# Cross-attention chain: softmax sums from TensorE and output division in the last four narrow jobs

## What is computed

```python
# layers 0 and 3
xn = rmsnorm(x, norm_w)
q = (xn @ wq).reshape(B, T, N_HEADS, HEAD_DIM)
k = (cond @ wk).reshape(B, S, N_KV_HEADS, HEAD_DIM)
v = (cond @ wv).reshape(B, S, N_KV_HEADS, HEAD_DIM)
scores = jnp.einsum('btgrd,bsgd->bgrts', qg, k) * scale
attn = jax.nn.softmax(scores.astype(jnp.float32), axis=-1).astype(q.dtype)
out = jnp.einsum('bgrts,bsgd->btgrd', attn, v).reshape(B, T, N_HEADS * HEAD_DIM)
return residual + out @ wo
```

## Time and profile before

| | us |
|---|---|
| median of 3 runs | 382.94 |
| lowest of them | 382.5 |
| profiled execution, its own time | 384.65 |
| span of the profiled execution | 382.9 |

### The profile page before, as it was taken

The page is one execution under the profiler, slowest core; times in us unless marked ns, Lnnn a source line. Parts: engine busy times, 40 slices in busy tenths (PEclk is TensorE's granted clock), DMA queues, the critical chain, the costliest instruction groups (busy, mean ns, idle before and its releaser), DMA issues.

```text
span 382.9 us, 10493 instructions
## 1 busy us (share of the span) xinstructions
PE 359.0 (94%) x3522; PEld 319.2 (83%) x3522; DVE 268.5 (70%) x1401; ACT 278.9 (73%) x1176; POOL 187.4 (49%) x220
## 2 busy tenths in 40 slices
PE   6799899999999999999999999999999999978655
PEld 6698698899989998989889988888999889867444
DVE  0999985564654566696888886667465775699982
ACT  3687998875575585657798999997666865647891
POOL 1576964552332245446576765443333435447661
PEclk9789999999999999999999999999999999999998
DMA  7915000000000000000000000000000000000000
GB/s 229 409 57 221 0 3 3 2 3 0 3 2 2 1 2 3 2 1 2 3 9 9 7 10 2 3 3 2 0 3 2 3 2 1 2 3 3 7 7 15
DMA packets 4739, 9.91 MB, mean 26 GB/s; under 512 B 592, under 2 KB 3024, under 8 KB 4432
## 3 DMA queue, kind: packets, MB, share of 16 engines
q1 hardware_dynamic: 4400, 8.99, 6.7%
q10 hardware_dynamic: 288, 0.27, 0.2%
HBM read 8.73 MB, written 0.52 MB: 24 GB/s over the span
## 4 chain that ended last, share of the span: by engine, by line
PE 74%; DVE 17%; ACT 5%; DMA 1%; issue 1%; SPq 0%; DVEq 0%
PE pt_ps L844 12%; PE scores_ps L831 9%; PE v_ps L895 8%; PE fill_ps L696 8%; PE q_ps L791 8%; PE v_ps L877 7%; PE fill_ps L697 7%; PE fill_ps L698 7%; DVE probs L609 7%; ACT probs L478 4%; PE v_ps L865 3%; DVE probsT L620 3%; PE q_ps L783 3%; DVE qn L592 2%; PE scores_ps L820 2%; DVE qn L588 2%
## 5 line engine op out<-in xcount | busy, mean ns | idle before, releaser
L478 ACT ACTIVATE probs<-probs,negmax 128x128 f32<-128x128 f32 x512 | 198.6, 391 | 82.5 <-DVE negmax L609 82.4
L375 POOL TENSOR_TENSOR probs<-probs,inv 128x512 f32<-128x512 f32 x128 | 137.3, 1076 | 178.2 <-DVE inv L616 177.8
L478 ACT ACTIVATION_READ_ACCUMULATOR probs<-probs,negmax 128x1 f32 x512 | 97.0, 190 | 0.0
L609 DVE CUSTOM_DVE_ANT_0 probs<-scores_ps,col_bias 128x128 f32<-128x128 f32 x256 | 58.1, 283 | 39.1 <-PE scores_ps L831 39.1
L844 PE MATMUL pt_ps<-smalls,probs 128*128 128x128 f32 x512 | 69.2, 278 | 7.5 <-DVE probsT L620 7.5
L844 PEld LDWEIGHTS pt_ps<-smalls,probs 128*128 128x128 f32 x512 | 56.6, 142 | 19.1 <-issue 15.8
L609 DVE CUSTOM_DVE_ANT_0 probs<-scores_ps,no_bias,inv_rms 128x128 f32<-128x128 f32 x224 | 64.3, 344 | 6.1 <-PE scores_ps L820 5.7
L620 DVE COPY probsT<-pt_ps 128x512 f32<-128x512 f32 x96 | 62.9, 683 | 2.7 <-PE pt_ps L844 0.6
L609 DVE DVE_READ_ACCUMULATOR2_ANT negmax<- 128x1 f32 x512 | 42.5, 83 | 0.0
L696 PE MATMUL fill_ps<-c_hi,w_hi 128*128 128x256 f32 x128 | 38.5, 301 | 0.0
L831 PE MATMUL scores_ps<-kT,qT 64*128 64x128 f32 x512 | 37.2, 285 | 0.0
(11 more groups left out here) (92 smaller groups left out, 586.0 us busy)
## 6 DMA issues: line engine op xcount, KB each, us to landing
kT<-in_kv_w SPq DMA_DIRECT2D x6, 512.0 KB, 6.9
w_qo<-in_qo_w SPq DMA_DIRECT2D x2, 1024.0 KB, 8.6
v<-in_ctxT SPq DMA_DIRECT2D x4, 256.0 KB, 9.9
v<-in_kv_w SPq DMA_DIRECT2D x2, 512.0 KB, 11.7
outT<-x SPq DMA_DIRECT2D x8, 64.0 KB, 1.6
wn<-in_narrow_w SPq DMA_DIRECT2D x1, 384.0 KB, 6.0
x<-in_xT SPq DMA_DIRECT2D x1, 384.0 KB, 8.5
oT<-in_narrow_kv ACTq DMA_DIRECT2D x1, 256.0 KB, 2.8
```

Of the source, the lines that this page charges most:

```text
L375: nc.gpsimd.tensor_tensor(p4, p4, inv[:, o % 2, side, :].unsqueeze(2).broadcast_to([P, 4, S]), ALU.mult,).then_inc(probs_made[side], 1)
L478: last = nc.scalar.activation(e, e, ACT.Exp, scale=-1.0, bias=negmax[:, o % 2, side, q:q + 1], accum_out=rowsum[:, o % 2, side, q:q + 1])
L609: last = nc.vector.tensor_tensor_reduce(out=probs[:, o % PROBS_RING, side, cols], in0=banks[scores_bank(o)][side][:, cols], in1=bias, scal ...
```

## The change

Jobs from LATE = 28 on work differently:

- The exponentials are no longer added up by ACT, their reciprocals are not taken per row, and POOL does not normalise. PE waits for `exps_made` instead of `probs_made` ahead of the transposes.
- `weighted_values` runs a second set of 16 products, with the new tile `sum_w` (ones in the place of the values) as weights. It gives, in `v_ps[:, T:2T]`, the sum of exponentials for each output element. DVE takes the 128 x 128 reciprocal of it into `oT[:, 1]`, waits for it, and multiplies the outputs by it on their way into `oT[:, 0]`.
- ACT copies both sides of `probsT` for halves 56 to 61: side 0 between its two groups of exponentials, side 1 behind the second. For halves 62 and 63 side 0 stays with DVE and side 1 with ACT.
- DVE's `scores_out` waits, from half 58 on, for the exponentials of two halves before.
- POOL makes `sum_w` at the start (a zeroing and a strided filling with ones).

```diff
@@ -76,2 +76,4 @@
 WIDE_ROWS = [(p, l) for p, l in ROWS if l not in NARROW]
+
+LATE = NJOBS - 4
 NARROW_ROWS = [(p, l) for p, l in ROWS if l in NARROW]
@@ -211,2 +213,4 @@
         v_narrow = sb("v_narrow", [P, 2, KV_HEADS * (PART + NARROW_D)])
+
+        sum_w = sb("sum_w", [P, KV_HEADS * (PART + NARROW_D)])
         qT = sb("qT", [P, IC, T])
@@ -248,3 +252,3 @@
         ones_made, zeros_made, setup_step, diagonals_made, bias_made = (
-            sem("ones_made"), sem("zeros_made"), sem("setup_step"), sem("diagonals_made"), sem("bias_made"))
+            sem("ones_made"), pair("zeros_made"), sem("setup_step"), sem("diagonals_made"), sem("bias_made"))
         sq_ready, rms_out, rms_made = sem("sq_ready"), sem("rms_out"), sem("rms_made")
@@ -259,2 +263,3 @@
         y_full, y_read = sem("y_full"), sem("y_read")
+        sum_w_made, sums_inverted = sem("sum_w_made"), sem("sums_inverted")
         out_stored = sem("out_stored")
@@ -271,2 +276,10 @@
 
+        def late(o):
+
+            return valid(o) and o // 2 >= LATE
+
+        def scalar_copies_both(o):
+
+            return late(o) and valid(o + 2)
+
         block = ctx.enter_context(nc.Block())
@@ -389,3 +402,3 @@
             def half(o):
-                if valid(o):
+                if valid(o) and not late(o):
                     normalise(o, 0)
@@ -412,4 +425,5 @@
             nc.gpsimd.memset(mean_w[:], 1.0 / C).then_inc(ones_made, 1)
-            nc.gpsimd.memset(v_narrow[:], 0.0).then_inc(zeros_made, 1)
-            pool.wait_ge(zeros_made, 1)
+            nc.gpsimd.memset(v_narrow[:], 0.0).then_inc(zeros_made[0], 1)
+            nc.gpsimd.memset(sum_w[:], 0.0).then_inc(zeros_made[1], 1)
+            pool.wait_ge(zeros_made[0], 1)
             square(0)
@@ -421,2 +435,4 @@
             split_context(1)
+            pool.wait_ge(zeros_made[1], 1)
+            nc.gpsimd.memset(sum_w.rearrange("p (g s) -> p g s", g=KV_HEADS)[:, :, 0:NARROW_D], 1.0).then_inc(sum_w_made, 1)
             for n, h in HALVES:
@@ -477,6 +493,15 @@
                     e = probs[:, o % PROBS_RING, side, q * S:(q + 1) * S]
-                    last = nc.scalar.activation(e, e, ACT.Exp, scale=-1.0, bias=negmax[:, o % 2, side, q:q + 1],
-                                                accum_out=rowsum[:, o % 2, side, q:q + 1])
+                    bias = negmax[:, o % 2, side, q:q + 1]
+                    if late(o):
+                        last = nc.scalar.activation(e, e, ACT.Exp, scale=-1.0, bias=bias)
+                    else:
+                        last = nc.scalar.activation(e, e, ACT.Exp, scale=-1.0, bias=bias,
+                                                    accum_out=rowsum[:, o % 2, side, q:q + 1])
                 last.then_inc(exps_made[side], 1)
 
+            def transposes_out(o, side):
+
+                act.wait_ge(pt_full[side], o + 1)
+                nc.scalar.activation(probsT[:, o % PROBST_RING, side, :], pt_ps[side][:], ACT.Copy).then_inc(pt_read[side], 1)
+
             def half(n, h):
@@ -492,7 +517,10 @@
                     exponentials(o, 0)
-                if scalar_copy(o - 2):
-                    act.wait_ge(pt_full[1], o - 1)
-                    nc.scalar.activation(probsT[:, (o - 2) % PROBST_RING, 1, :], pt_ps[1][:], ACT.Copy).then_inc(pt_read[1], 1)
+                if scalar_copies_both(o - 2):
+                    transposes_out(o - 2, 0)
+                elif scalar_copy(o - 2):
+                    transposes_out(o - 2, 1)
                 if valid(o):
                     exponentials(o, 1)
+                if scalar_copies_both(o - 2):
+                    transposes_out(o - 2, 1)
                 for name in FILLS.get(o, [])[:1]:
@@ -605,2 +633,4 @@
                     dve.wait_ge(rms_made, narrow_index(n) + 1)
+                if late(o - 2):
+                    dve.wait_ge(exps_made[side], o - 1)
                 dve.wait_ge(scores_full[side], o + 1)
@@ -623,3 +653,7 @@
                 dve.wait_ge(v_full, uses(n, h))
-                if is_narrow(n):
+                if n >= LATE:
+                    nc.vector.reciprocal(oT[:, 1, :], v_ps[:, T:2 * T]).then_inc(sums_inverted, 1)
+                    dve.wait_ge(sums_inverted, n - LATE + 1)
+                    nc.vector.tensor_tensor(oT[:, 0, :], v_ps[:, 0:T], oT[:, 1, :], ALU.mult).then_inc(v_read, 1)
+                elif is_narrow(n):
                     nc.vector.tensor_copy(oT[:, 0, :], v_ps[:, 0:T]).then_inc(v_read, 1)
@@ -648,3 +682,3 @@
                     scores_out(o, 0)
-                if valid(o - 1):
+                if valid(o - 1) and not late(o - 1):
                     inverse_sums(o - 1, 1)
@@ -658,3 +692,4 @@
                 if valid(o - 2):
-                    transposes_out(o - 2, 0)
+                    if not scalar_copies_both(o - 2):
+                        transposes_out(o - 2, 0)
                     if not scalar_copy(o - 2):
@@ -838,3 +873,6 @@
                 for side in range(2):
-                    pe.wait_ge(probs_made[side], o + 1)
+                    if late(o):
+                        pe.wait_ge(exps_made[side], o + 1)
+                    else:
+                        pe.wait_ge(probs_made[side], o + 1)
                     if o > 0:
@@ -862,8 +900,13 @@
                     pe.wait_ge(vn_made, i + 1)
-                    for g in range(KV_HEADS):
-                        for r in range(REP):
-                            last = nc.tensor.matmul(v_ps[PART * r:PART * (r + 1), 0:T],
-                                                    v_narrow[:, i % 2, PART * g:PART * (g + 1)],
-                                                    probsT[:, (o - 1 + r // 2) % PROBST_RING, r % 2, g * T:(g + 1) * T], start=(g == 0),
-                                                    stop=(g == KV_HEADS - 1))
+                    products = [(0, v_narrow[:, i % 2])]
+                    if n >= LATE:
+                        pe.wait_ge(sum_w_made, 1)
+                        products.append((T, sum_w[:]))
+                    for first, blocks in products:
+                        for g in range(KV_HEADS):
+                            for r in range(REP):
+                                last = nc.tensor.matmul(v_ps[PART * r:PART * (r + 1), first:first + T],
+                                                        blocks[:, PART * g:PART * (g + 1)],
+                                                        probsT[:, (o - 1 + r // 2) % PROBST_RING, r % 2, g * T:(g + 1) * T],
+                                                        start=(g == 0), stop=(g == KV_HEADS - 1))
                     last.then_inc(v_full, 1)
```

## The result

| | before | changed |
|---|---|---|
| median, us | 382.72 (4 runs) | 396.03 (4 runs, 393.22 to 397.27) |
| ratio | 1 | 1.034, 95% interval 1.027 to 1.041 |
| span of the profiled execution | 382.9 | 395.5 |
| mean granted clock in it | 0.987 | 0.969 |

The four executions of the kernel before took 382.50, 382.50, 382.94 and 452.04 us; the ratio leaves the last, slow one out. The changed kernel is slower by 3.4%, 13.3 us by the medians. The forecast was 392.9 us with a range up to 396; the median lies just beyond that upper end.

A forecast was written before the change was run, and what follows sets the result against it. Late jobs were taken as bound by a ring of hand-overs between four engines, not TensorE. Laps +1.7, +2.5, +5.5, less 0.4, gave +9.3; low clock +0.65, total +10.0 on 382.94: 392.9 us, range 388.5 to 396.

The forecast's parts named there:

- half 56 to 59: Stretch before half 59: DVE, the busy engine there, loses 0.4 us of reciprocals.
- A: From the first score instruction of half 59 to that of half 61: 10.55 us against 8.85, +1.7.
- B: From the first score instruction of half 61 to that of half 63: 9.67 us against 7.16, +2.5.
- C: From half 63's first score instruction to the end: 18.0 us against 13.83, or 12.5 at full clock: +5.5.
- The ring: Halves 56 to 63 run in hand-overs between four engines; scores through reciprocal sum to 8.57 us, added time not hidden.
- Exponentials without a read: ACT, late halves: without eight accumulator reads, exponentials step 0.29 us instead of 0.38; four take 1.17 us, not 1.54.
- The added products: PE, late jobs: 16 more matmuls per job lie on the path, 1.0 us per job.
- The reciprocal: DVE's 128x128 reciprocal out of PSUM ahead of the output product: 1.24 us each, at 8.5 ns a column.
- The low clock: PE's reduced clock, 1.35 us of the last lap before, returns there and slows 16 added matmuls too: +0.65 us.
- The rival that priced it: Reduced clock spans laps B and C, making products, transposes and projection dearer: up to 396.5 us; chance 12%.
- The cheap reciprocal: Rival: DVE's 128x128 reciprocal takes 0.32 us instead of 1.24, four cost 3.7 us less: 389.2 us; chance 15%.
- The freed engines: Rival: outputs of jobs 28 to 30 fall into slack, ACT's reduced work sets the laps: 380.5 us; chance 8%.

The follow-up runs named there:

- small fills: Changed kernel plus filling matmuls on constants, 3 to 8 in each place where TensorE waits in the late jobs; 391.85 us, ratio 1.022.
- all the removals: Kernel before without accumulator reads, row-sum reciprocals and normalisation in the last four jobs, nothing added, outputs not divided; 381.08 us, ratio 0.995.
- sums first: Changed kernel, but in jobs 29 to 31 TensorE makes the sums first, into q_ps, and DVE divides during the weighted values; 391.60 us, ratio 1.024.
- before with fills: Kernel before plus filling matmuls on constants, 2 to 8 in each place where TensorE waits in the late jobs; 383.38 us, ratio 0.999.
- both copies alone: Kernel before with ACT copying both sides of probsT for halves 56 to 61, side 1 behind the second group of exponentials; 390.19 us, ratio 1.018.
- first fills: Changed kernel plus 10 to 24 matmuls on constants in each TensorE wait of the late jobs; 413.40 us, ratio 1.079.

## Why the prediction was right in kind and short by 3 us

| lap | predicted | changed | at full clock (small fills) |
|---|---|---|---|
| half 56 to 59 | -0.4 to before | 15.60 (before 15.84: -0.2) | 15.58 |
| A | 10.55 | 12.00 | 10.35 |
| B | 9.67 | 12.18 | 9.54 |
| C | 18.0, +0.65 clock | 19.45 | 17.58 |

- **The ring.** Right. DVE waits for the products ahead of each reciprocal, ACT's second copy gates the transposes of side 1, and at full clock each lap comes out within 0.5 us of its sum, and within 0.2 us once the reciprocal's measured price is put in (10.27, 9.39, 17.4).
- **Exponentials without a read.** Right: 0.29 us apart, four in 1.17 us in the chain. Little comes of it: all the removals together bring 2.2 us.
- **The added products.** Right in place, 0.87 us each at full clock for the 1.0 put in.
- **The reciprocal.** The step that took the whole excess of 34 ns of the 128x4 instruction as time per column overshot: 0.96 us, not 1.24. Four times 0.28 us, 1.1 us too much. The Trainium skill (VectorE: DVE Perf Modes, First, the fixed hardware budget) has Reciprocal as an iterative divide with a repeat count of 8; the trace agrees in so far as the columns count. The prediction's reading of it as 8 cycles a column does not hold: by the clock of 0.96 GHz that the Trainium skill gives (VectorE: DVE Perf Modes, Specifications), 6.3 ns a column is an estimated 6 cycles.
- **The low clock.** The step that failed. It was put at +0.65 us over the 1.35 us of before, 2.0 in all, on the ground that with a busy share of 0.6 and gaps of about 2 us the clock had held until 372 us. In the changed kernel's profile it cost 6.2 us, and it fell in lap A already, then through laps B and C. The rival that priced it (up to 396.5) had been given 12%. What took its place: the clock fell behind much shorter waits than the 2.22 us of before, and whether it falls there varies. The changed kernel and "sums first" run the same instructions until half 60, with the same two waits of 0.81 and 1.02 us ahead of the products of job 28. The clock fell at 357 us in the one and not before 366 in the other, whose busy time (columns as in the earlier trace rows) is:

```profile
356.00:360.00 4.00, 2.51 (x68) 2.10 (x68) 1.37 (x9) 4.00 (x13) 0.21 (x1) 1.00 0.02 4
...
364.00:368.00 4.00, 1.53 (x8) 1.15 (x8) 2.94 (x22) 4.00 (x14) 0.00 (x0) 0.74 0.00 0
```

- **The sum.** The laps from half 56 on add up to 59.23 us against 45.68 of before: +13.55, where +10.0 was forecast. The reciprocal takes off 1.1. The low clock rose from 1.05 (13.83 less 12.78 of before with fills) to 6.2, by 5.1 instead of 0.65, which adds 4.5: 10.0 - 1.1 + 4.5 = 13.4. With both kernels filled, at full clock, the laps differ by 53.05 - 44.63 = 8.4 us; the prediction's terms, with the measured reciprocal and no clock, give 9.3 - 1.1 = 8.2. The ring was priced right, the clock not. That the total missed by only 3 us is partly luck: the reciprocal was 1.1 us too dear and covered that much of what the clock was too cheap.
- **Other rivals.** The cheap reciprocal (0.32 us) is refuted by 0.96. The freed engines do not win: DVE waits for the products in each of the four jobs.
- **Two smaller terms.** Taking away DVE's reciprocals before half 59 gave 0.24 us, not 0.4. The low clock of before costs 1.05 us of lap C, not 1.35.

What stays open: what exactly lets the clock fall at one gap and not at the next. No run here isolates it.

## What to carry to other kernels

Where engines hand work to each other in a ring, price an edit by its place between two hand-overs; the idle shares said nothing here, and a copy moved behind four exponentials cost more than it freed elsewhere. Price the low clock of TensorE with every lengthening of a ring in which it already waits: what waited longer here often ran slower afterwards, and with both copies alone that more than doubled the loss (6.9 us, of which an estimated 2.9 are hand-overs). Before dividing a large tile to spare the division of a small one, count columns: the small reciprocal here was 4 columns, the new one 128.

## What the runs showed of the hardware that was not expected

- A matmul of 32 columns repeated on the same 32 rows of PSUM takes 0.23 us in float32; the products, which go round the four groups of 32 output rows, take 0.07 us each at the same shape. A transpose of 128 columns, another kind of matmul, takes 0.13 us (eight in 1.07). The likely reading is that the products overlap across the four groups; the fills also differ in using the same weights and output rows each time, and no run takes the two apart.
- More work on TensorE made the kernel faster: with 0.235 us fills in its waits the laps of the changed kernel lost 6.2 us. With 16 products per job taken away the granted clock in the profile was lower, 0.958 in the mean, and lap C gained only 0.24 us for two sets of 0.87; that the one caused the other is not shown.
- The reciprocal of float32 on VectorE costs 6.3 ns a column, 958 ns for 128x128.
- The start of the program varies by up to 3.6 us between the profiled executions. The wait for the first transfer accounts for 1.5 us of it. Behind it the same instructions take different times: DVE's `wn_lo<-oT,wn_hi` took 1.75 us in before and 0.68 in before with fills, its `c_lo<-v,c_hi` 1.12 us there and 2.31 in the first fills, where the clock was also at 0.50 from 9 to 12 us. Differences under 1% between medians are hard to read without the laps.
